# Storing six normed blocks to DRAM by row scatters in a gated-expert and mixer kernel

## What is computed

```python
x = L0_attn_x                                   # (16, 256, 128)
xn = _layernorm(x, axis=-1)
s = _L0_attn_ref(xn, ...)                       # projections, scan over time, group norm, gate
...
for r in range(R):                              # R = 4, the expert branch
    logits = flat @ Wg[r] + bg[r]
    vals, idx = jax.lax.top_k(logits, TOPK)     # 2 of 4 experts
    w = jax.nn.softmax(vals, axis=-1)
    hmid = jax.nn.gelu(jnp.einsum('nh,ehf->enf', flat, W1) + b1[:, None, :])
    y = jnp.einsum('enf,efh->enh', hmid, W2) + b2[:, None, :]
    out = jnp.einsum('ne,enh->nh', cw, y)
    cur = cur + out.reshape(b, s, h)
...
x = x + s * _silu(cur)
```

## Time and profile before

| | us |
|---|---|
| median of 2 runs | 784.92 (784.88 to 784.97) |
| span of the profiled execution | 782.9 |
| PE busy | 777.2 (99%) |
| DVE busy | 689.3 (88%) |
| ACT busy | 641.1 (82%) |
| POOL busy | 115.2 (15%) |
| software-driven DMA queue, share of 16 engines | 25.8% |
| SP's DMA queue, share of 16 engines | 19.5% |

### The profile page before, as it was taken

The page is one execution under the profiler, slowest core; times in us unless marked ns, Lnnn a source line. Parts: engine busy times, 40 slices in busy tenths (PEclk is TensorE's granted clock), DMA queues, the critical chain, the costliest instruction groups (busy, mean ns, idle before and its releaser), DMA issues.

```text
span 782.9 us, 9951 instructions
## 1 busy us (share of the span) xinstructions
PE 777.2 (99%) x3392; PEld 619.2 (79%) x3392; DVE 689.3 (88%) x1096; ACT 641.1 (82%) x873; POOL 115.2 (15%) x141
## 2 busy tenths in 40 slices
PE   8999999999999999999999999999999999999998
PEld 6778788887888878888788887888877788888887
DVE  7999987899888889879899788987988989988998
ACT  7989888787888877888788877887877878888886
POOL 0122111111111111111111111111111111111110
PEclk9999999999999999999999999999999999999999
DMA  8467572332642416333154322643227434655453
GB/s 267 139 132 182 128 208 50 95 95 41 148 89 62 107 28 163 92 64 88 33 157 107 81 57 41 149 108 96 41 41 175 108 56 107 134 123 122 70 117 71
DMA packets 77010, 81.62 MB, mean 104 GB/s; under 512 B 48800, under 2 KB 54688, under 8 KB 72992
## 3 DMA queue, kind: packets, MB, share of 16 engines
q0 software_dynamic: 18624, 34.61, 25.8%
q1 hardware_dynamic: 57920, 46.11, 19.5%
q10 hardware_dynamic: 416, 0.26, 0.1%
HBM read 41.91 MB, written 3.93 MB: 59 GB/s over the span
## 4 chain that ended last, share of the span: by engine, by line
PE 95%; ACT 2%; DVE 2%; issue 0%; DMA 0%; DVEq 0%
PE h_bank L1079 15%; PE h_bank L1080 15%; PE h_bank L1083 15%; PE y_bank L1152 15%; PE y_bank L1142 15%; PE y_bank L1140 14%; PE p_bank L1079 2%; PE p_bank L1083 2%; PE p_bank L1080 2%; PE r_bank L1189 1%; ACT g L465 1%; ACT g_hi L471 1%; DVE g_lo L759 0%; DMA cur<-in_x 0%; DVE stats L600 0%
## 5 line engine op out<-in xcount | busy, mean ns | idle before, releaser
L465 ACT ACTIVATE g<-h_bank,b_c 128x512 f32<-128x512 f32 x512 | 329.3, 682 | 77.8 <-PE h_bank L1083 77.0
L759 DVE TENSOR_TENSOR g_lo<-g,g_hi 128x1024 fp32r<-128x1024 f32 x256 | 310.0, 1222 | 72.8 <-ACT g_hi L471 71.2
L471 ACT ACTIVATE g_hi<-g 128x1024 fp32r<-128x1024 f32 x256 | 271.8, 1062 | 8.1
L415 POOL DMA_DIRECT2D cur<-tmp x126 | 110.6, 878 | 642.4 <-DVE tmp L773 544.1
L1079 PE MATMUL h_bank<-cur_hi,w_hi 128*128 128x512 f32 x512 | 202.9, 396 | 0.2 <-ACT cur_hi L513 0.2
L1083 PE MATMUL h_bank<-cur_lo,w_hi 128*128 128x512 f32 x512 | 202.2, 395 | 0.0
L1080 PE MATMUL h_bank<-cur_hi,w_lo 128*128 128x512 f32 x512 | 202.1, 395 | 0.0
L1140 PE MATMUL y_bank<-g_hi,w_hi 128*128 128x512 f32 x504 | 196.2, 393 | 0.0
L1142 PE MATMUL y_bank<-g_hi,w_lo 128*128 128x512 f32 x488 | 193.6, 397 | 0.0
L1152 PE MATMUL y_bank<-g_lo,w_hi 128*128 128x512 f32 x504 | 137.9, 395 | 0.1
L1079 PEld LDWEIGHTS h_bank<-cur_hi,w_hi 128*128 128x128 f32 x512 | 96.2, 188 | 26.6 <-issue 3.8
(11 more groups left out here) (153 smaller groups left out, 410.5 us busy)
## 6 DMA issues: line engine op xcount, KB each, us to landing
cur<-tmp POOLq DMA_DIRECT2D x126, 256.0 KB, 3.3
cw_b<-cw_scratch SPq DMA_DIRECT2D x31, 1024.0 KB, 5.2
xn_t<-cur SPq DMA_DIRECT2D x8, 256.0 KB, 3.1
cur<-in_x SPq DMA_DIRECT2D x7, 256.0 KB, 5.0
xr<-in_x SPq DMA_DIRECT2D x28, 64.0 KB, 3.4
out<-o SPq DMA_DIRECT2D x28, 64.0 KB, 2.1
xn_scratch<-o POOLq DMA_DIRECT2D x6, 256.0 KB, 3.0
xr<-xn_scratch SPq DMA_DIRECT2D x24, 64.0 KB, 2.5
```

The source lines that it names most:

```text
L415: pool.dma_start(cur[:, block_of(s // E)], tmp[:, s % SUMS, :], accum_op=ALU.add).then_inc(summed, DMA)
L465: nc.scalar.activation(g[:, gb, ft * BLK:(ft + 1) * BLK], hb[ft][:, :], ACT.Gelu_apprx_tanh, bias=b1_c[:, e * FT + ft:e * FT + ft + 1]).th ...
L471: nc.scalar.activation(g_hi[:, gb, h], g[:, gb, h], ACT.Copy).then_inc(g_hi_done, 1)
L759: nc.vector.tensor_tensor(g_lo[:, gb, h], g[:, gb, h], as_f32(g_hi[:, gb, h]), ALU.subtract).then_inc(g_lo_done, 1)
```

## The change

The scratch tensor becomes a flat list of 3072 rows of 512 bytes. POOL makes a table of row numbers once (`row[p, b, t]` = 512 b + 4 p + t). Each store of a block becomes four scatters: scatter t takes the columns of `xn_st` of tile t (128 partitions x 512 bytes, 64 KB) and puts partition p's row where `row[p, b, t]` says. Every wait on `xn_saved` of a block goes from 16 to 64. Addresses and contents are the same as before, and so are the loads that follow.

```diff
+        row = sb("row", [128, NB - BY_PE, TPB], i32)
...
+        rows_made = sem("rows_made")
...
-        xn_scratch = nc.dram_tensor("xn_scratch", (NB - BY_PE, BLK, D), f32, kind="Internal").ap()
+        xn_scratch = nc.dram_tensor("xn_scratch", ((NB - BY_PE) * BLK, D), f32, kind="Internal").ap()
...
-                sp.wait_ge(xn_saved[b - BY_PE], DMA)
+                sp.wait_ge(xn_saved[b - BY_PE], DMA * TPB)
...
-                                 turned(xn_scratch[b - BY_PE], c)).then_inc(xn_staged[q], DMA)
+                                 turned(xn_scratch[(b - BY_PE) * BLK:(b - BY_PE + 1) * BLK, :], c)).then_inc(xn_staged[q], DMA)
...
+            pool.iota(row[:, :, :], pattern=[[BLK, NB - BY_PE], [1, TPB]], base=0, channel_multiplier=TPB).then_inc(rows_made, 1)
+            pool.wait_ge(rows_made, 1)
...
-                    pool.dma_start(xn_scratch[b - BY_PE].rearrange("(p t) d -> p t d", t=TPB),
-                                   xn_st[:, b % 2, :].rearrange("p (t d) -> p t d", t=TPB)).then_inc(xn_saved[b - BY_PE], DMA)
+                    for t in range(TPB):
+                        pool.indirect_dma_start(out=xn_scratch,
+                                                out_offset=bass.IndirectOffsetOnAxis(ap=row[:, b - BY_PE, t:t + 1], axis=0),
+                                                in_=xn_st[:, b % 2, t * D:(t + 1) * D], in_offset=None,
+                                                bounds_check=(NB - BY_PE) * BLK - 1).then_inc(xn_saved[b - BY_PE], DMA)
...
-                    act.wait_ge(xn_saved[b - BY_PE - 2], DMA)
+                    act.wait_ge(xn_saved[b - BY_PE - 2], DMA * TPB)
...
-                    dve.wait_ge(xn_saved[b - BY_PE - 2], DMA)
+                    dve.wait_ge(xn_saved[b - BY_PE - 2], DMA * TPB)
```

## The result

The changed kernel took 800.59 us (median, 800.27 to 800.90) against 784.92 before: 15.7 us more, a ratio of 1.0202 (95% interval 1.0172 to 1.0231). The profiled execution's span went from 782.9 to 798.8 us, 15.9 more. The forecast was 795.5 us in a range from 787 to 805, with the larger chance on "within 2%"; the measurement lies on that border.

The account below looks back on a forecast made before the run. PE was taken to bound the kernel, so its waits add in full: 9.5 us by the second place (holding the first's 5.4) plus 1.1 at the third, 10.6 in all, giving 795.5 us, range 787 to 805.

Parts of the forecast that it names:

- within 2%: Outcome class for the whole kernel: a change of under 15.7 us, which measurement cannot tell from none; chance 0.72.
- What bounds the kernel: PE, busy 777.2 of 782.9 us: whatever makes it wait is added to the end in full.
- The table and the larger counts: Row table made on POOL while it waits at the start, and larger wait counts: both costed at nothing.
- Nothing here can make the kernel faster: Whole kernel: PE's 5.7 idle us lie mostly outside the change; a chance of 0.01 was left for faster.
- The price of a scatter: POOL's time per scatter, called p: 1.15 us, from plain store 0.57 plus two extras of 0.29; range 0.57 to 1.72.
- the dear rival: Scatter with p above 1.47, over 2% slower, chance 0.27; in one form (0.05) each waits out DVE's subtraction, 815 us.
- p above 1.47: Case of a scatter costing POOL over 1.47 us, making the kernel slower by over 2%; chance 0.27.
- First place: Block 3: store 2's delay passes through the accumulates to store 3; logits wait 4.6 us, PE is 5.4 late.
- Second place: Gates of turn 2, queued on SP behind block 4's loads, delay `combine(8)`; PE 9.5 us late at `down(10)`.
- store 4 moves with DVE: In the second place: accumulate 6 waits for DVE, so store 4 behind it starts 7.37 us later, at 67.96.
- 12p - 4.3: PE's lateness in us at `down(10)`, from twelve scatters of blocks 2 to 4 at p each; 9.5 at 1.15.
- Third place: Block 7, placed at 99.6 when PE wants it for `logits(2)` at 98.5: 1.1 us more, 4p - 3.5 where positive.

Follow-up runs that it names:

- e11: Kernel before with only an unused tensor of 384 bytes per partition allocated behind `warm`, moving `cur_hi` and all behind it; 771.35 us against 785.35.
- e12: Changed kernel with an unused tensor of 288 bytes per partition, so `cur_hi` lies 384 bytes further on than in the kernel before; 787.46 us against 785.35.
- e4: Changed kernel with only blocks 2 to 4 stored by scatters, the others by one plain store each; 800.15 us against 784.67 for the kernel before.
- e7: Changed kernel with store 3 ahead of accumulate 2 on POOL rather than behind it; 799.20 us against 784.95 for the kernel before.
- e9: Kernel before with 14 small chained memsets on POOL ahead of each plain store, their spare tensor moving tensors behind it; 780.76 us against 785.21.
- e6: Changed kernel with `spread_gates(2)` ahead of `load_staged(4)` on SP; 803.05 us against 784.95 for the kernel before.
- e1: Changed kernel with each of the 24 scatters replaced by a plain store of the same 64 KB; 791.34 us against 784.67 for the kernel before.
- e3: Changed kernel with only blocks 5 to 7 stored by scatters, the others by one plain store each; 791.99 us against 784.67 for the kernel before.
- e8: Changed kernel with both store 3 ahead of accumulate 2 and `spread_gates(2)` ahead of `load_staged(4)`; 798.37 us against 784.95 for the kernel before.

## Why the prediction was right or wrong

**What bounds the kernel: right.** Every microsecond that PE was made late stayed.

**The table and the larger counts: right as to work, but not as to nothing.** POOL made the table in 0.18 us under cover. Its 96 bytes moved the operands of PE, and the drift of 0.9 us is of the kind that e11 and e12 show; that it is exactly this table's is likely, since e4 with the same table has it too, but the changed kernel wasn't run with zero shift. "Nothing here can make the kernel faster" was argued without this: e11 is 14.0 us faster by an unused tensor alone.

**The price of a scatter: too low, 1.15 against 1.54 us.** The parts are 1.0 for the scatter, 0.3 of gap between two, and on average 0.25 for DVE's subtractions that some wait out. The row of the accumulate (0.86) gave the order of the first; no row had the gap. The form of the dear rival in which each scatter waits out a subtraction was right as a mechanism, but 7 of 24 were longer than 1.1 us, not all. By that figure this was the case "p above 1.47", to which 0.27 was given. At 1.54 the sum of the prediction gives 14.2 + 2.7 = 16.9 us, and 15.7 were measured, but this agreement is luck: the 16.9 would be lateness by `logits(2)` at full clock, while the 15.9 us of the spans are 11.6 by `down(10)` and 4.3 of clock, drift and a late wait that the sum does not have.

**First place: right.** Block 3 back at 59.31 (forecast 58.13), PE 5.9 late at the logits (4.6), and accumulate 2 as the carrier (e7). e9 shows that POOL's time does it without any scatter.

**Second place: the delay right, the path half right.** 9.5 was forecast with p = 1.15 and 11.6 measured. `combine(8)` did wait for the gates. But block 4 is as late as they are (e6), and POOL's chain of accumulates holds store 4 back on its own when DVE doesn't (e7). The prediction took "store 4 moves with DVE" as the whole of it. The formula 12p - 4.3 itself did not hold. The twelve scatters on this path took 1.50 us each with their gaps, for which it gives 13.7, and 11.6 came: the landings were 1.3 us after the last issue rather than 2.2, at block 3 and at block 4, and the broadcast landed after 4.5 rather than 5.0. In e9 it gives 8.9 for 7.0. In e1 it erred the other way, 2.5 us for 5.2, in part by the slower write of the gates. The errors in p and in the landings partly cancelled.

**Third place: 1.1 forecast, 0 measured.** It exists (e3), but PE was late enough by itself, in part by its clock.

**What was missing: the clock.** The prediction said PE's busy time would not change. It grew by 7.4 us, of which 5.25 came because after each of the two waits PE ran at half clock for 5 to 6 us. Behind the second wait that added 2.9 us to the path; behind the first it added 2.35 that the wait at the second place then covered.

Of the difference of about 5 us between 795.5 and 800.6, the clock makes 2.9, the drift 0.9 and the wait at 615 us 0.5; the rest is 2.1 us more at `down(10)`, from the dearer scatter less the quicker landings, and 1.1 less at the third place.

## What to carry to other kernels

An issue of 128 pieces on POOL cost the same with a quarter of the bytes (other numbers of pieces weren't tried); splitting one transfer into four, or giving it a list, is paid in POOL's time, and in the time of everything that is queued behind it there. When a chain of waits is priced, look for the second chain of nearly the same length (here the accumulates beside DVE, block 4 beside the gates): moving one of them gave back little or made it worse. A wait of PE like those of 2.8 us and more seen here must be priced with slower matmuls behind it, and a new tensor, however small, moves all that is allocated after it, which here is worth nearly as much as the whole change (14.0 against 15.7 us).

## What the runs showed of the hardware that was not expected

- A scatter of 128 rows takes POOL 0.98 to 1.1 us whether a row is 512 bytes or 2 KB, with 0.30 us of idle time ahead of it. A plain store of 64 KB in a row of four takes 0.53 to 0.62, like one of 256 KB.
- A scatter issued while DVE subtracts one SBUF tensor from another ends 0.85 to 0.90 us after that instruction's end, up to 2.0 us in all, and 3.05 when it waits out two. Plain issues (0.53 to 0.62 us) and accumulating ones (0.85 to 1.01) showed no such wait. The scatter of 1.20 us in the changed kernel ended 0.87 us after DVE's rounding of `cur`, which has one input, so the subtractions may not be the only such instructions; this was not tried.
- After waits of PE of 2.8 to 7.8 us (14 of them in nine kernels) the granted clock was at 1.2 GHz, and it was back at 2.4 after 3.2 to 6.1 us of matmuls. Behind waits of 1.8 us (e7) and 2.1 us (e8) it stayed at 2.4.
- Four loads of 64 KB issued 0.8 us behind a broadcast of 1 MB on the same queue were back after 8.65 us instead of 4.34.
- Moving PE's moving operands, and all else that is allocated behind, by 384 bytes per partition made the kernel 14 us faster; moves of 32, 96 and 160 bytes went with drifts of 0.7 to 3.4 us the other way. Which tensor it is, and by what rule, was not tried.
